# Two homes for turned blocks, rounding steps in rows with gaps, and small operations taken tile by tile

## The chip, the cores and the metric

The kernel runs on one core of a Trainium2 chip. Five engines work side by side, each through its own list of instructions: TensorE (PE; its weight loads are listed as PEld), VectorE (DVE), ScalarE (ACT), GpSimd (POOL) and SyncE (SP), which here issues the DMAs. They wait for one another through semaphores. The metric is the device time of one execution in microseconds; lower is better.

## The reference

Four batches of 256 tokens with 256 features go through four residual stages. In plain form:

```
x = x + xattn0(layernorm(x), ctx, Wq, bq, Wk, bk)      # softmax over ctx, one head
x = x + ternary_ffn(layernorm(x), w_norm, w_gv, w_out)
x = x + xattn1(layernorm(x), ctx, mask, Wq, Wk, Wv, Wo) # 16 heads of 128, 256 keys
x = x + fp8_ffn(layernorm(x), gate, up, down, scales)   # weights rounded to float8_e4m3

# ternary_ffn: weights to {-1, 0, 1} by their mean, activations to 8 bits by their row maximum
scale = 127 / max(max(abs(x)), EPS);  q = clip(round(x * scale), -128, 127) / scale
# fp8_ffn: silu(x @ r(gate) * gs) * (x @ r(up) * us) @ r(down) * ds,  r(w) = w.astype(float8_e4m3fn)
```

## The kernel before, in words

The tokens lie in 8 tiles of 128 rows, two to a batch. Every engine's instructions are issued in an order that is written out by hand as a list of calls; semaphores set what waits for what, and nothing is scheduled by a program.

**The second attention** goes in 32 passes; a pass is one pair of heads of one batch. Its products are split into a high and a low part in a 32-bit format, so that each takes three matmuls (`product`, which records L2016). In a pass TensorE makes queries (`queries`: products of `xT` and `m`), scores (`ctx` and `q`), the product with values (`contexts`: `pT` or `tp` and `cr`) and the output (`attn_out`: `n` and `oT`). VectorE makes the low parts (`q_lo` L1551, `oT_lo` L1595), masks the scores and finds their minimum (L1564), and turns the probabilities; ScalarE takes exponentials and the high parts; POOL normalises and, for the turned passes, subtracts `tp_lo` (L667).

**Turning the probabilities.** In passes 3 to 29 the probabilities get from rows to columns in two steps. VectorE transposes blocks of 32x32 from `sm` to `blocks` (L1581). SP writes `blocks` to a room in DRAM in four DMAs (`blocks_written`, L442) and reads it back as `tp` in two, one for each half of the keys (`blocks_read`, L455; the same issues appear as L454 where a wait is listed). In SP's queue a pass's write and read stand behind those of the pass before. `turns_before(n)` counts the turned passes ahead of pass n; `block_room` and `tp` have two rooms, `blocks` has one. The other passes use TensorE's transposes.

**Rounding to fp8.** The weights are rounded in 16 pieces of 288 columns, spread over the second attention. VectorE takes the exponent bits (L1601) and makes a step of them (L1604); POOL adds the step, subtracts it, and corrects (L672 to L680).

**Small operations.** For each batch the statistics give a mean and a variance for each of its two tiles: one column each, side by side. `stats` negates the means (L1410), `variances` and `second_stats` add an epsilon (L1413, L1461, L1462), `scaled` works out the 8-bit scales of the ternary layer (L1489 to L1495, five dependent steps) and applies them to `gbuf` (L1498), which the first gate product (L2085) waits for. All of them handle both columns in one instruction.

## Time and profile before

| | |
|---|---|
| Median of 3 runs | 310.96 us (310.67 to 313.23) |
| The profiled execution's own time | 312.58 us |
| Its span, first to last instruction | 310.5 us |
| TensorE busy | 293.6 us (95%) |
| VectorE busy | 260.9 us (84%) |
| ScalarE busy | 253.7 us (82%) |
| POOL busy | 218.5 us (70%) |
| Mean granted TensorE clock | 0.995 of 2.4 GHz |

The span counts from the first to the last instruction of the profiled execution; the rest of its time lies around it. Busy shares are means over stages with different limits, so a stage's own stretch has to be read. "Idle before" is put down to what ended last. Matmul records overlap: their ends are modelled, and the distance between two starts is what a step takes in dense work. A few matmul records can be missing.

### The profile page before, as it was taken

What the parts mean: (1) busy time and instruction counts of PE and PEld (TensorE: products, weight loads), DVE (VectorE), ACT (ScalarE), POOL (GpSimd) and SP (SyncE); (2) the same over time, 40 slices, a digit from 0 to 9 for tenths busy, and PEclk for the clock granted to TensorE, in tenths of its full rate; (3) what the DMA queues carried; (4) which work ended last, traced back from release to release, by engine and by line L of the source; (5) the groups of instructions that cost most, each with busy time, mean ns of one, the idle gap of its engine ahead of it and who ended that gap; (6) DMA issues with size and microseconds to landing.
All of it is one profiled execution on the core that took longest, in us unless ns stands there. A gap on an engine that the chain in (4) does not pass through costs nothing.

```text
span 310.5 us, 6396 instructions
## 1 busy us (share of the span) xinstructions
PE 293.6 (95%) x1980; PEld 259.9 (84%) x1992; DVE 260.9 (84%) x713; ACT 253.7 (82%) x603; POOL 218.5 (70%) x290
## 2 busy tenths in 40 slices
PE   3968999999999999999999999999999999999994
PEld 2755487798989998979889999999988999899884
DVE  3959999999999999889999986997768897675665
ACT  2398995598999998979999899778899999855460
POOL 3558864556998578999879998886678798952001
PEclk9979999999999999999999999999999999999999
DMA  7996032001326548885878756537645647200103
GB/s 223 367 381 199 35 101 70 1 8 30 93 47 189 157 138 251 220 212 139 228 210 226 199 144 174 161 108 219 182 144 148 179 143 211 68 3 0 36 1 101
DMA packets 54609, 44.59 MB, mean 144 GB/s; under 512 B 11696, under 2 KB 45104, under 8 KB 54576
## 3 DMA queue, kind: packets, MB, share of 16 engines
q1 hardware_dynamic: 54016, 43.93, 49.0%
q10 hardware_dynamic: 560, 0.26, 0.3%
q8 instruction: 16, 0.26, 0.3%
q14 instruction: 17, 0.14, 0.2%
HBM read 27.01 MB, written 15.20 MB: 136 GB/s over the span
## 4 chain that ended last, share of the span: by engine, by line
PE 59%; DVE 20%; DMA 8%; issue 5%; SPq 4%; ACT 2%; DVEq 0%
PE pb L2016 41%; DMA block_room<-blocks 5%; PE pb L2279 5%; PE pb L2314 4%; DMA wraw<-in_wgvT 3%; DVE blocks L1581 3%; SPq L442 2%; DVE sm L1564 2%; PE pb L2130 2%; PE pb L2091 2%; PE pb L2076 2%; DVE wraw L1455 2%; DVE step L1601 1%; PE pb L2227 1%; DVE q_lo L1551 1%
## 5 line engine op out<-in xcount | busy, mean ns | idle before, releaser
L667 POOL TENSOR_TENSOR tp_lo<-tp,pT_hi 128x512 fp32r<-128x512 f32 x54 | 70.0, 1311 | 15.1 <-ACT pT_hi L993 14.8
L981 ACT ACTIVATE sm<-sm,smin 128x256 f32<-128x256 f32 x128 | 63.6, 501 | 4.7 <-DVE smin L1564 4.4
L1564 DVE CUSTOM_DVE_ANT_0 sm<-pb,mask_all 128x256 f32<-128x256 f32 x128 | 47.3, 418 | 5.6 <-PE pb L2016 5.5
L1581 DVE STREAM_TRANSPOSE blocks<-sm 128x1024 f32<-128x1024 f32 x27 | 33.5, 1240 | 7.4 <-DMA block_room<-blocks 7.0
L2016 PE MATMUL pb<-ctx_hi,q_hi 128*128 128x256 f32 x128 | 38.1, 298 | 1.1 <-DVE q_lo L1551 0.6
L662 POOL TENSOR_SCALAR sm<-sm,srec 128x256 f32<-128x256 f32 x64 | 30.5, 488 | 10.4 <-DVE srec L1570 10.4
L2016 PE MATMUL pb<-xT_hi,m_hi 128*128 128x256 f32 x128 | 37.3, 292 | 0.3 <-DVE xT_lo L1540 0.3
L2016 PE MATMUL pb<-n_hi,oT_hi 128*128 128x256 f32 x128 | 37.1, 290 | 0.2 <-DVE oT_lo L1595 0.2
L2016 PE MATMUL pb<-xT_hi,m_lo 128*128 128x256 f32 x128 | 36.2, 283 | 0.0
L2016 PE MATMUL pb<-xT_lo,m_hi 128*128 128x256 f32 x128 | 36.2, 283 | 0.0
L2016 PE MATMUL pb<-ctx_lo,q_hi 128*128 128x256 f32 x128 | 36.2, 282 | 0.0
L2016 PE MATMUL pb<-ctx_hi,q_lo 128*128 128x256 f32 x128 | 36.1, 282 | 0.0
L2016 PE MATMUL pb<-n_hi,oT_lo 128*128 128x256 f32 x128 | 36.1, 282 | 0.0
L2016 PE MATMUL pb<-n_lo,oT_hi 128*128 128x256 f32 x128 | 36.1, 282 | 0.0
L993 ACT ACTIVATE pT_hi<-tp 128x512 fp32r<-128x512 f32 x54 | 31.7, 622 | 2.4 <-PE pb L2016 2.3
L999 ACT ACTIVATE sm<-sm,srec 128x256 f32<-128x256 f32 x64 | 29.0, 504 | 3.3 <-DVE srec L1570 3.3
L583 POOL TENSOR_TENSOR rstd<-ve,nhalf 128x2 f32<-128x2 f32 (+1 forms) x16 | 13.2, 826 | 21.6 <-DVE ve L1413 18.3
L2016 PEld LDWEIGHTS pb<-ctx_hi,q_hi 128*128 128x128 f32 x128 | 24.4, 191 | 3.6 <-DVE q_lo L1551 2.1
L2016 PE MATMUL pb<-pT_hi,cr_hi 128*128 128x512 f32 x64 | 26.5, 415 | 0.5 <-DVE pT_lo L1591 0.5
L2016 PEld LDWEIGHTS pb<-n_hi,oT_hi 128*128 128x128 f32 x128 | 24.4, 191 | 1.7 <-DVE oT_lo L1595 0.6
L2016 PEld LDWEIGHTS pb<-xT_hi,m_hi 128*128 128x128 f32 x128 | 24.5, 191 | 1.5 <-DVE xT_lo L1540 0.5
L2016 PE MATMUL pb<-pT_hi,cr_lo 128*128 128x512 f32 x64 | 25.3, 395 | 0.0
(195 smaller groups left out, 943.0 us busy)
## 6 DMA issues: line engine op xcount, KB each, us to landing
block_room<-blocks SPq DMA_DIRECT2D x108, 128.0 KB, 2.8
tp<-block_room SPq DMA_DIRECT2D x54, 256.0 KB, 3.0
w_raw<-in_w SPq DMA_DIRECT2D x4, 576.0 KB, 4.6
wraw<-in_wgvT SPq DMA_DIRECT2D x4, 512.0 KB, 8.4
wraw<-in_woutT SPq DMA_DIRECT2D x2, 512.0 KB, 9.3
out<-xb SPq DMA_DIRECT2D x4, 256.0 KB, 2.2
xa<-in_x SPq DMA_DIRECT2D x3, 256.0 KB, 4.5
xb<-in_ctxT SPq DMA_DIRECT2D x2, 256.0 KB, 5.1
```

The costliest lines, as they stand in the source:

```text
L442: sp.dma_start(rows[:, :, i * P:(i + 1) * P], blocks[32 * i:32 * (i + 1), :, :, :].rearrange("a g k b -> a g (k b)")).then_inc(blocks_out, 16)
L583: g.tensor_tensor(rstd[:, planes, tiles(b)], ve[:, planes, tiles(b)], nhalf[:, planes, tiles(b)], ALU.pow).then_inc(rstd_done, 1)
L662: g.tensor_scalar(sm[:, n % 2, k, :], sm[:, n % 2, k, :], srec[:, n % 2, k:k + 1], 1.0, ALU.mult, ALU.mult).then_inc(norm_done, 1)
L667: g.tensor_tensor(tp_lo[:, z, c, :], tp[:, z, c, :], as_f32(pT_hi[:, c, :]), ALU.subtract).then_inc(pT_lo_pool, 1)
L981: a.activation(sm[:, n % 2, k, :], sm[:, n % 2, k, :], ACT.Exp, bias=smin[:, n % 2, k:k + 1], scale=-1.0, accum_out=ssum[:, n % 2, k:k + 1 ...
L993: a.activation(pT_hi[:, c, :], whole, ACT.Copy).then_inc(pT_hi_done, 1)
L999: a.activation(sm[:, n % 2, k, :], sm[:, n % 2, k, :], ACT.Identity, scale=srec[:, n % 2, k:k + 1]).then_inc(norm_act, 1)
L1564: v.tensor_tensor_reduce(out=sm[:, n % 2, k, :], in0=bank(passing_bank("s", 2 * n + h))[:, (k % 2) * S:(k % 2 + 1) * S], in1=mask_all[:, b ...
L1581: v.transpose(blocks[:].rearrange("p g k b -> p k g b"), sm[:, n % 2, :, :].rearrange("p k (g b) -> p k g b", b=32)).then_inc(blocks_done, 1)
L2016: last = t_.matmul(dst, a_, b_, start=start and k == 0, stop=stop and k == n - 1, skip_group_check=check)
L2279: last = t_.matmul(dst, weight[:, k, i * P:(i + 1) * P], part[:, k, tok], start=n == 0, stop=n == 2 * KD - 1)
L2314: last = t_.matmul(bank(DOWN[h][n])[:, t * D:(t + 1) * D], part[:, i, rows], down8[:, i, :], start=i == 0 and t == 0 and part is f_hi, sto ...
```

## The change

- **Turned blocks.** The transposes alternate between `blocks` (even turns) and another room (odd turns): `gbuf` of the ternary layer for the turns before the 17th, and then `uq`, read as 32-bit words. The semaphore of the writes is split in two, one for each room; a transpose waits for the writes of two turns ago, the first odd one for the last use of `gbuf`, the 17th for the last transposes out of `uq`. The two semaphores of the reads become one: SP issues a turn's two reads after both of the turn before have landed, and ScalarE's copies wait for both halves. The first copy of an fp8 gate also waits for the last write out of `gbuf`.
- **Rounding.** `sum8` becomes three rows of 96 columns with one column of gap behind each. VectorE writes the exponent bits there rather than to `step8`, and makes the step from there; POOL's four operations take the same three rows.
- **Small operations.** Those on two columns become two on one column each, 52 more instructions in all; in `scaled`, two tensor-by-tensor products take the second operand as a pointer to one value a row, and the maximum with EPS moves into the first of them. The reciprocal stays on two columns.

```diff
-        sum8 = tile(ctx, "sum8", [P, PIECE])[:]
+        sum8 = tile(ctx, "sum8", [P, 3, PIECE // 3 + 1])[:, :, 0:PIECE // 3]
...
-        blocks_done, blocks_out = sem("blocks_done"), sem("blocks_out")
-        blocks_in = [sem(f"blocks_in{c}") for c in range(SC)]
+        blocks_done, blocks_in = sem("blocks_done"), sem("blocks_in")
+        blocks_out = [sem(f"blocks_out{z}") for z in range(2)]
...
+        UQ_TURN = 17
...
+        def thirds(piece):
+            return piece.rearrange("p (a n) -> p a n", a=3)
...
+        def turned_blocks(k):
+            if k % 2 == 0:
+                return blocks[:]
+            if k < UQ_TURN:
+                return gbuf[:].rearrange("p z t d -> p (z t d)").rearrange("p (g k b) -> p g k b", k=4, b=32)
+            return as_f32(uq[:].rearrange("p a d -> p (a d)")).rearrange("p (g k b) -> p g k b", k=4, b=32)
...
             def blocks_written(n):
...
                 if k >= 2:
-                    sp.wait_ge(blocks_in[0], 16 * (k - 1))
-                    sp.wait_ge(blocks_in[1], 16 * (k - 1))
+                    sp.wait_ge(blocks_in, 16 * SC * (k - 1))
...
-                    sp.dma_start(rows[:, :, i * P:(i + 1) * P], blocks[32 * i:32 * (i + 1), :, :, :].rearrange("a g k b -> a g (k b)")).then_inc(blocks_out, 16)
+                    sp.dma_start(rows[:, :, i * P:(i + 1) * P], turned_blocks(k)[32 * i:32 * (i + 1), :, :, :].rearrange("a g k b -> a g (k b)")).then_inc(blocks_out[k % 2], 16)
...
             def blocks_read(n):
...
-                sp.wait_ge(blocks_out, 64 * (k + 1))
+                sp.wait_ge(blocks_out[k % 2], 64 * (k // 2 + 1))
+                if k >= 1:
+                    sp.wait_ge(blocks_in, 16 * SC * k)
                 for c in range(SC):
-                    if k >= 1:
-                        sp.wait_ge(blocks_in[c], 16 * k)
-                    sp.dma_start(tp[:, k % 2, c, :], block_room[k % 2 * S + c * P:k % 2 * S + (c + 1) * P, :]).then_inc(blocks_in[c], 16)
+                    sp.dma_start(tp[:, k % 2, c, :], block_room[k % 2 * S + c * P:k % 2 * S + (c + 1) * P, :]).then_inc(blocks_in, 16)
...
-                g.tensor_tensor(sum8, raw, step8, ALU.add).then_inc(sum8_done, 1)
+                g.tensor_tensor(sum8, raw, thirds(step8), ALU.add).then_inc(sum8_done, 1)
...
             def probs(n, c):
                 if by_blocks(n):
-                    act.wait_ge(blocks_in[c], 16 * (turns_before(n) + 1))
+                    act.wait_ge(blocks_in, 16 * SC * (turns_before(n) + 1))
...
-                v.tensor_scalar(nmean[:, sl], mv[:, sl, 0], -1.0, None, ALU.mult)
+                for t in range(sl.start, sl.stop):
+                    v.tensor_scalar(nmean[:, t:t + 1], mv[:, t, 0:1], -1.0, None, ALU.mult)
...
             def variances(sl, done):
-                v.tensor_scalar(ve[:, 0, sl], mv[:, sl, 1], EPS, None, ALU.add).then_inc(done, 1)
+                for t in range(sl.start, sl.stop):
+                    ins = v.tensor_scalar(ve[:, 0, t:t + 1], mv[:, t, 1:2], EPS, None, ALU.add)
+                ins.then_inc(done, 1)
...
             def scaled(b):
...
-                scale_next(v.tensor_tensor(hmax[:, sl], hmax[:, sl], rstd[:, 1, sl], ALU.mult))
-                scale_next(v.tensor_scalar(hstep[:, sl], hmax[:, sl], EPS, 1.0 / 127.0, ALU.max, ALU.mult))
+                each = [slice(t, t + 1) for t in range(sl.start, sl.stop)]
+                for one in each:
+                    scale_part(v.tensor_scalar(hmax[:, one], hmax[:, one], rstd[:, 1, one], EPS, ALU.mult, ALU.max))
+                dve.wait_ge(scale_step, scale_count[0])
+                for one in each:
+                    scale_part(v.tensor_scalar(hstep[:, one], hmax[:, one], 1.0 / 127.0, None, ALU.mult))
+                dve.wait_ge(scale_step, scale_count[0])
                 scale_next(v.reciprocal(hrec[:, sl], hstep[:, sl]))
-                scale_next(v.tensor_tensor(hqs[:, sl], hrec[:, sl], rstd[:, 1, sl], ALU.mult))
+                for one in each:
+                    scale_part(v.tensor_scalar(hqs[:, one], hrec[:, one], rstd[:, 1, one], None, ALU.mult))
+                dve.wait_ge(scale_step, scale_count[0])
...
-                if k >= 1:
-                    dve.wait_ge(blocks_out, 64 * k)
-                elif n >= 1:
+                if k >= 2:
+                    dve.wait_ge(blocks_out[k % 2], 64 * (k // 2))
+                elif k == 1:
+                    dve.wait_ge(hq_done, B - 1)
+                else:
                     dve.wait_ge(oT_ps, n)
-                v.transpose(blocks[:].rearrange("p g k b -> p k g b"), sm[:, n % 2, :, :].rearrange("p k (g b) -> p k g b", b=32)).then_inc(blocks_done, 1)
+                if k == UQ_TURN:
+                    for z in range(2):
+                        dve.wait_ge(uq_turned[z], 16 * (NT // 2 - 1))
+                v.transpose(turned_blocks(k).rearrange("p g k b -> p k g b"), sm[:, n % 2, :, :].rearrange("p k (g b) -> p k g b", b=32)).then_inc(blocks_done, 1)
...
-                v.tensor_scalar(step8.bitcast(I32), w8_raw[:, n * PIECE:(n + 1) * PIECE].bitcast(I32), 0x7F800000, None,
+                v.tensor_scalar(sum8.bitcast(I32), thirds(w8_raw[:, n * PIECE:(n + 1) * PIECE]).bitcast(I32), 0x7F800000, None,
                                 ALU.bitwise_and).then_inc(exp8_done, 1)
                 dve.wait_ge(exp8_done, 2 * n + 1)
-                v.tensor_scalar(step8, step8, FP8_LEAST, FP8_STEP, ALU.max, ALU.mult).then_inc(exp8_done, 1)
+                v.tensor_scalar(thirds(step8), sum8, FP8_LEAST, FP8_STEP, ALU.max, ALU.mult).then_inc(exp8_done, 1)
```

The order of TensorE, ScalarE and POOL is as before. On VectorE, where the scales of the first batch are worked out (`hmax`, `hstep`, `hrec`, `hqs`, `gsc`: one column for each tile), it reads before:

```order
L1489 TENSOR_TENSOR hmax<-hmax,rstd 128x2 [waits rstd2_done,gmax_done]
L1490 TENSOR_SCALAR hstep<-hmax 128x2 [waits scale_step]
L1491 RECIPROCAL hrec<-hstep 128x2 [waits scale_step]
L1492 TENSOR_TENSOR hqs<-hrec,rstd 128x2 [waits scale_step]
L1495 TENSOR_SCALAR gsc<-hstep,wmean 128x2 [waits wmean_done,scale_step]
L1498 TENSOR_SCALAR gbuf<-gbuf,hqs 128x256 x2
```

and now:

```order
L1510 TENSOR_SCALAR hmax<-hmax,rstd 128x1 [waits rstd2_done,gmax_done]
L1510 TENSOR_SCALAR hmax<-hmax,rstd 128x1
L1513 TENSOR_SCALAR hstep<-hmax 128x1 [waits scale_step]
L1513 TENSOR_SCALAR hstep<-hmax 128x1
L1515 RECIPROCAL hrec<-hstep 128x2 [waits scale_step]
L1517 TENSOR_SCALAR hqs<-hrec,rstd 128x1 [waits scale_step]
L1517 TENSOR_SCALAR hqs<-hrec,rstd 128x1
L1522 TENSOR_SCALAR gsc<-hstep,wmean 128x1 [waits wmean_done,scale_step]
L1522 TENSOR_SCALAR gsc<-hstep,wmean 128x1
L1526 TENSOR_SCALAR gbuf<-gbuf,hqs 128x256 x2
```

Four of the five steps are now pairs, and each step still waits for the one before. On VectorE where pass 4 is turned (`step`, `sum`: the rounding; `blocks`: the turned block; `q_lo`: low part of the next queries), before:

```order
L1410 TENSOR_SCALAR nmean<-mv 128x2 [waits mv_done]
L1413 TENSOR_SCALAR ve<-mv 128x2
L1601 TENSOR_SCALAR step<-w_raw 128x288 [waits w8_done,ld_eight0]
L1604 TENSOR_SCALAR step<-step 128x288 [waits exp8_done]
L1581 STREAM_TRANSPOSE blocks<-sm 128x4x8x32 [waits blocks_out,norm_done,norm_act]
L1551 SCALAR_TENSOR_TENSOR q_lo<-pb,q_hi 128x512 [waits q_hi_done]
```

and now:

```order
L1422 TENSOR_SCALAR nmean<-mv 128x1 [waits mv_done]
L1422 TENSOR_SCALAR nmean<-mv 128x1
L1426 TENSOR_SCALAR ve<-mv 128x1 x2
L1634 TENSOR_SCALAR sum<-w_raw 128x3x96 [waits w8_done,ld_eight0]
L1637 TENSOR_SCALAR step<-sum 128x288 [waits exp8_done]
L1614 STREAM_TRANSPOSE gbuf<-sm 128x4x8x32 [waits hq_done,norm_done,norm_act]
L1579 SCALAR_TENSOR_TENSOR q_lo<-pb,q_hi 128x512 [waits q_hi_done]
```

The transpose stands at the same place, writes `gbuf` and waits for the ternary layer's `hq_done` rather than for the block's write; later ones wait for `blocks_out0` and `blocks_out1` in turn. SP's queue around the same pass, write and read, before:

```order
L442 DMA block_room<-blocks 32x8x128 [waits blocks_done]
L442 DMA block_room<-blocks 32x8x128 x3
L455 DMA tp<-block_room 128x512 [waits blocks_out,blocks_in0,hq_turned,base_done]
L455 DMA tp<-block_room 128x512 [waits blocks_in1]
L442 DMA block_room<-blocks 32x8x128 [waits blocks_in1,blocks_in0,blocks_done]
L442 DMA block_room<-blocks 32x8x128 x3
L455 DMA tp<-block_room 128x512 [waits blocks_in0,blocks_out,oT_ps]
```

and now:

```order
L452 DMA block_room<-gbuf 32x8x128 [waits blocks_done]
L452 DMA block_room<-gbuf 32x8x128 x3
L465 DMA tp<-block_room 128x512 [waits blocks_out1,blocks_in,hq_turned,base_done]
L465 DMA tp<-block_room 128x512
L452 DMA block_room<-blocks 32x8x128 [waits blocks_in,blocks_done]
L452 DMA block_room<-blocks 32x8x128 x3
L465 DMA tp<-block_room 128x512 [waits blocks_in,blocks_out0,oT_ps]
```

The DMAs keep their order; both reads are released at once, and the next write still stands behind them.

## Rows read from the trace of the kernel before

**Rows 1.** The page, part 1: busy time, share and instructions of each engine.

```profile
PE 293.6 (95%) x1980; PEld 259.9 (84%) x1992; DVE 260.9 (84%) x713; ACT 253.7 (82%) x603; POOL 218.5 (70%) x290
```

**Rows 2.** The page, part 4: the chain that ended last, by engine.

```profile
PE 59%; DVE 20%; DMA 8%; issue 5%; SPq 4%; ACT 2%; DVEq 0%
```

**Rows 3.** Stretches: start:end, length, busy us (x instructions) by engine, PEclk, DMA share, GB/s.

```profile
20.00:76.00 56.00, 53.70 (x351) 42.25 (x352) 53.54 (x148) 47.75 (x94) 36.55 (x52) 0.99 0.26 82
110.00:206.00 96.00, 94.31 (x672) 85.78 (x677) 86.59 (x251) 86.72 (x227) 85.13 (x108) 1.00 0.71 195
206.00:236.00 30.00, 30.00 (x212) 28.05 (x211) 22.94 (x69) 25.94 (x67) 21.79 (x29) 1.00 0.56 157
236.00:242.00 6.00, 5.67 (x35) 4.86 (x34) 5.35 (x7) 5.97 (x16) 4.95 (x6) 1.00 0.60 187
242.00:300.00 58.00, 58.00 (x381) 52.68 (x381) 41.93 (x97) 42.50 (x95) 32.68 (x40) 1.00 0.27 78
```

**Rows 4.** Timeline of TensorE at 122 us: start us, us, operation [idle before <-releaser].

```profile
121.71 0.28 PE L2016 MATMUL pb<-xT_hi,m_lo 128*128 128x256 f32 x1
122.19 0.39 PE L2016 MATMUL pb<-ctx_hi,q_hi 128*128 128x256 f32 x1 [0.20 <-DVE q_lo L1551]
122.42 0.28 PE L2016 MATMUL pb<-ctx_lo,q_hi 128*128 128x256 f32 x1
```

**Rows 5.** Waits of the weight loads: total us, times, longest.

```profile
PEld pb L2016 <- DVE q_lo L1551: 2.1, 4, 0.9
```

**Rows 6.** Waits of VectorE, the transpose.

```profile
DVE blocks L1581 <- DMA block_room<-blocks: 7.0, 9, 1.9
```

**Rows 7.** Waits of SP's queue, the reads.

```profile
SPq L454 <- DMA block_room<-blocks: 33.7, 17, 3.2
```

**Rows 8.** Timeline of SP's queue, the last turn's two reads.

```profile
264.38 0.81 SPq L455 DMA_DIRECT2D tp<-block_room  x2
```

**Rows 9.** VectorE by line: shapes, count, busy us, mean ns, idle before.

```profile
L1601 DVE TENSOR_SCALAR step<-w_raw 128x288 int32<-128x288 int32 x16 | 11.3, 707 | 0.8 <-POOL w8r L680 0.8
L1604 DVE TENSOR_SCALAR step<-step 128x288 f32<-128x288 f32 x16 | 10.4, 649 | 0.6
L1404 DVE BATCH_NORM_STATS2 bnst<-xa 128x6 f32<-128x256 f32 x16 | 5.9, 412 | 4.1 <-DMA xa<-in_x 4.1
L1595 DVE TENSOR_TENSOR oT_lo<-pb,oT_hi 128x512 fp32r<-128x512 f32 x32 | 21.6, 676 | 3.8 <-ACT oT_hi L1005 3.8
```

**Rows 10.** Timelines of VectorE and POOL around 118 us.

```profile
118.29 1.28 DVE L1604 TENSOR_SCALAR step<-step 128x288 f32<-128x288 f32 x1
...
116.80 2.60 POOL L667 TENSOR_TENSOR tp_lo<-tp,pT_hi 128x512 fp32r<-128x512 f32 x2
```

**Rows 11.** POOL, two lines: ns least/median/most, first and last start, shapes.

```profile
L633 POOL TENSOR_SCALAR xa<-gbuf x3: 617/617/617, 38.1 to 77.9; 128x512 bf16<-128x512 f32 x3
...
L639 POOL CAST n_hi<-n_raw x8: 602/610/616, 39.8 to 90.6; 128x512 fp32r<-128x512 f32 x8
```

**Rows 12.** Timeline of VectorE: small operations that start apart.

```profile
25.07 0.17 DVE L1410 TENSOR_SCALAR nmean<-mv 128x2 f32<-128x2 f32 x1
25.15 0.16 DVE L1461 TENSOR_SCALAR ve<-mv 128x2 f32<-128x2 f32 x1
...
43.17 0.20 DVE L1524 TENSOR_SCALAR osc<-ucl,wmean 128x1 f32<-128x1 f32 x1
43.30 0.20 DVE L1521 TENSOR_SCALAR ucl<-umax,gsc 128x1 f32<-128x1 f32 x1
```

**Rows 13.** VectorE, three small lines: ns least/median/most, starts, shapes.

```profile
L1492 DVE TENSOR_TENSOR hqs<-hrec,rstd x4: 160/180/936, 29.9 to 73.9; 128x2 f32<-128x2 f32 x4
...
L1495 DVE TENSOR_SCALAR gsc<-hstep,wmean x4: 228/228/981, 30.1 to 74.8; 128x2 f32<-128x2 f32 x4
...
L1521 DVE TENSOR_SCALAR ucl<-umax,gsc x8: 196/205/216, 42.6 to 178.3; 128x1 f32<-128x1 f32 x8
```

**Rows 14.** Waits of TensorE, the first gate product.

```profile
PE pb L2085 <- DVE gbuf L1498: 0.4, 1, 0.4
```

More of the change, by code:

```diff
@@ L669, in eighths @@
             def eighths(n):
-                raw = w8_raw[:, n * PIECE:(n + 1) * PIECE]
+                raw = thirds(w8_raw[:, n * PIECE:(n + 1) * PIECE])
                 pool.wait_ge(exp8_done, 2 * n + 2)
-                g.tensor_tensor(sum8, raw, step8, ALU.add).then_inc(sum8_done, 1)
+                g.tensor_tensor(sum8, raw, thirds(step8), ALU.add).then_inc(sum8_done, 1)
             def eighths_out(n):
                 pool.wait_ge(sum8_done, n + 1)
-                g.tensor_tensor(sum8, sum8, step8, ALU.subtract).then_inc(step8_done, 1)
+                g.tensor_tensor(sum8, sum8, thirds(step8), ALU.subtract).then_inc(step8_done, 1)
                 pool.wait_ge(step8_done, 2 * n + 1)
-                g.tensor_scalar(step8, sum8, FP8_OVER, 0.0, ALU.mult, ALU.mult).then_inc(step8_done, 1)
+                g.tensor_scalar(thirds(step8), sum8, FP8_OVER, 0.0, ALU.mult, ALU.mult).then_inc(step8_done, 1)
                 pool.wait_ge(step8_done, 2 * n + 2)
-                g.tensor_tensor(w8r[:, n * PIECE:(n + 1) * PIECE], sum8, step8, ALU.add).then_inc(w8_done, 1)
+                g.tensor_tensor(thirds(w8r[:, n * PIECE:(n + 1) * PIECE]), sum8, thirds(step8), ALU.add).then_inc(w8_done, 1)
             def rows4(b):
@@ L1014, in gate4_copy @@
                     act.wait_ge(ld_scales, 48)
+                    act.wait_ge(blocks_out[1], 64 * (UQ_TURN // 2))
                 act.wait_ge(g4_ps, c + 1)
@@ L1460, in second_stats @@
                 stats(xa, sl)
-                v.tensor_scalar(ve[:, 0, sl], mv[:, sl, 1], EPS, None, ALU.add)
-                v.tensor_scalar(ve[:, 1, sl], mv[:, sl, 1], 1.0 + EPS, EPS * EPS, ALU.mult, ALU.add).then_inc(ve2_done, 1)
+                for t in range(sl.start, sl.stop):
+                    v.tensor_scalar(ve[:, 0, t:t + 1], mv[:, t, 1:2], EPS, None, ALU.add)
+                    ins = v.tensor_scalar(ve[:, 1, t:t + 1], mv[:, t, 1:2], 1.0 + EPS, EPS * EPS, ALU.mult, ALU.add)
+                ins.then_inc(ve2_done, 1)
             def centred(b):
@@ L1478, in _, with scale_part, scale_next @@
             scale_count = [0]
-            def scale_next(ins):
+            def scale_part(ins):
                 scale_count[0] += 1
                 ins.then_inc(scale_step, 1)
+            def scale_next(ins):
+                scale_part(ins)
                 dve.wait_ge(scale_step, scale_count[0])
@@ L1488, in scaled @@
                 dve.wait_ge(rstd2_done, b + 1)
-                scale_next(v.tensor_tensor(hmax[:, sl], hmax[:, sl], rstd[:, 1, sl], ALU.mult))
-                scale_next(v.tensor_scalar(hstep[:, sl], hmax[:, sl], EPS, 1.0 / 127.0, ALU.max, ALU.mult))
+                each = [slice(t, t + 1) for t in range(sl.start, sl.stop)]
[5 more added lines that the diff above has]
+                dve.wait_ge(scale_step, scale_count[0])
                 scale_next(v.reciprocal(hrec[:, sl], hstep[:, sl]))
-                scale_next(v.tensor_tensor(hqs[:, sl], hrec[:, sl], rstd[:, 1, sl], ALU.mult))
+                for one in each:
+                    scale_part(v.tensor_scalar(hqs[:, one], hrec[:, one], rstd[:, 1, one], None, ALU.mult))
+                dve.wait_ge(scale_step, scale_count[0])
                 if b == 0:
                     dve.wait_ge(wmean_done, 1)
-                v.tensor_scalar(gsc[:, sl], hstep[:, sl], wmean[:, 0:1], None, ALU.mult).then_inc(gsc_done, 1)
+                for one in each:
+                    ins = v.tensor_scalar(gsc[:, one], hstep[:, one], wmean[:, 0:1], None, ALU.mult)
+                ins.then_inc(gsc_done, 1)
                 for t in range(TB):
@@ L1589, in probs_low @@
                 if n == LAST_TURNED + 1 and c == 0:
-                    dve.wait_ge(blocks_out, 64 * turns_before(n))
+                    dve.wait_ge(blocks_out[0], 64 * ((turns_before(n) + 1) // 2))
                 v.tensor_tensor(pT_lo[:, c, :], bank(passing_bank("pT", SC * n + c)), as_f32(pT_hi[:, c, :]), ALU.subtract).then_inc(pT_lo_done, 1)
```

## The prediction

> **What bounds the kernel now.** I read the page's first list, then its chain of waits, then the busy time by stretches, then the timeline of TensorE and VectorE inside the stretches that lose time. The first list shows TensorE busy for 95% of the span and VectorE, the next, for 84% [rows 1]. The chain that ended last runs over TensorE for 59% and over VectorE for 20% [rows 2]. So TensorE is the bound, and VectorE is what sometimes holds it up. The stretches say where [rows 3]. From 206 to 236 us TensorE is busy for 30.00 of 30, from 242 to 300 for 58.00 of 58: nothing can be won there by freeing another engine. From 110 to 206 us it idles 96.00 − 94.31 = 1.69 us, from 236 to 242 another 0.33: 2.02 us together. From 20 to 76 us it idles 2.30 us while VectorE is busy for 53.54 of 56: there VectorE is nearly full.
>
> A busy row hides part of a stall, since matmul records overlap. In dense work one 128x256 step starts every 0.12 us. At 121.71 the last dense one starts, the next at 122.19 with 0.20 us shown as idle and VectorE's q_lo as the releaser, and the one behind it at 122.42: 0.71 us for what takes 0.24, so 0.47 is lost where 0.20 is shown [rows 4]. I counted nine such gaps between 110 and 242 us; with 0.2 hidden in each the loss is 2.02 + 9 × 0.2 = 3.8 us. The list of waits names q_lo first for the weight loads of the products, 2.1 us [rows 5]; q_lo stands on VectorE right behind the block transpose and the rounding. **So about 3.8 us is what the change can return after 110 us**, however much time VectorE saves.
>
> **Part 1, alternate buffers.** The 27 transposes wait 7.0 us in nine cases for the DRAM writes to have read the one buffer [rows 6]. With two buffers a transpose waits for the writes of two passes ago, which are a whole pass old; these 7.0 us go from VectorE. TensorE cannot have paid all of it, since its whole loss there is 3.8 us. What is late next is SP. Its read of a turn stands in its queue behind the landing of the same turn's write, where it already spends 33.7 us in 17 waits [rows 7], so the next write can still not be issued before. The loop of SP stays as long as it was; the wait leaves VectorE's queue, where q_lo, oT_lo and the scores stood behind it, and stays in SP's, where only the next transfers stand behind it. The two reads of a turn are now released together and ScalarE waits for both. They are issued 0.4 us apart in one pair of 0.81 us [rows 8]: 0 where ScalarE is later than that anyway, 0.4 us once at worst (the last turn). I take 0.
>
> The rooms reused are dead by then, so the first odd turns and the turn that goes to uq wait for work that ended many passes before. The extra wait of the fp8 gate copy is for a write some passes old. Both 0.
>
> **Part 2, the rounding.** The two VectorE steps of a piece take 11.3 + 10.4 = 21.7 us in 32 instructions, 0.707 and 0.649 us in the mean [rows 9]. Many are stretched: the step at 118.29 lasts 1.28 us and ends with POOL's pair of subtractions that runs from 116.80 to 119.40 [rows 10]. The written or read tile now has three rows of 96 with a gap. Bounds for such a step: below, that nothing changes, 0.68 in the mean; above, that it goes at one element per cycle and is no longer held by POOL. The nearest rows of that kind are the statistics of 256 columns, 0.412 us, and the subtraction of 512, 0.676 [rows 9], which never stretch: 0.412 + 32/256 × 0.264 = 0.445 us for 288. I take this, because these rows are nearest in size and the change alters just the shape of the rows that stretch: 32 × 0.445 = 14.2 us, so **−7.5 us on VectorE**; the other end is 0. POOL's three-row forms cost it nothing: its 128x512 step that reads with gaps takes 617 ns, one without 610 [rows 11].
>
> The Trainium skill says the same of the cause in "SBUF — State Buffer", section "Who interferes with whom": VectorE's two-port modes and GpSimd exclude each other on a shared port. Its "VectorE: DVE Perf Modes", section "What auto-detection actually checks", makes that mode hang on outermost counts that are even or equal; 288 against 3 is neither. The stretched row agrees with the first; no row before shows the second.
>
> **Part 3, small operations by tiles.** 52 operations on two columns become 104 on one, so 52 more. Independent ones start 0.08 us apart (25.07, 25.15), those that take a pointer 0.13 (43.17, 43.30) [rows 12]. 40 are of the first kind, 12 of the second, and eight tensor-tensor ones become pointer ones at 0.05 more: 40 × 0.075 + 12 × 0.13 + 0.4 = **+5.0 us on VectorE**. What is removed is their stretching: from the two rows whose longest is furthest above their median, 0.936 − 0.180 and 0.981 − 0.228 make 1.5 us, while the one-column operation stays between 196 and 216 ns in all eight [rows 13]. Between 20 and 76 us lie, for each of four batches, 0.225 in the statistics and 0.49 in the scales, and 0.15 once: +3.0 us, less the 1.5. That is +1.5 on VectorE where it is nearly full. TensorE's idle time there is shared with ScalarE, so I put **+0.5 us** on the path; the ends are −1.5 (only the stretches counted) and +3.0. In the tail, the last statistics are 0.15 later, behind matmuls without a gap [rows 3]: 0.
>
> A rule speaks against this part. The rows show starts 0.08 apart for operations that last 0.17. The Trainium skill, "VectorE: DVE Perf Modes", section "The DRAIN you can't avoid", has the next operation wait until the pipe is empty; by that the 52 would cost 52 × 0.17 = 8.8 us rather than 5.0, as an estimate.
>
> **The sum.** On VectorE −7.0 − 7.5 + 5.0 and the small stretches: about −11 of 260.9 us. On the path, of the 3.8 us after 110 us I take seven tenths, 2.7, because VectorE also waits for ScalarE (3.8 us before oT_lo alone [rows 9]) and would wait there longer. So −2.7 + 0.5 = **−2.2 us**. The profiled execution took 312.58 us for a span of 310.5, the median of the three runs is 310.96; I take the 2.2 from the median: **308.8 us**, 307.3 to 309.9 if the mechanism holds (all of the 3.8 with 0.2 for the early part, or half of it with 0.8).
>
> **The rivals.**
> - *More returns* (18%): all 3.8 us go, and the freed stretches return some 0.7 in the early stage too, where the scales' chain holds TensorE. 310.96 − 4.5 = 306.5. For it: q_lo heads the list of waits. Against: +1.5 on a full VectorE.
> - *TensorE waits for others* (22%): VectorE is free, but the same gaps are then ended by ScalarE, POOL or SP. Between 236 and 242 ScalarE is busy for 5.97 of 6 [rows 3], and SP's loop is not shortened. 311.0.
> - *The gapped step does not do it* (8%): it runs and stretches as before, and only the second buffer works. The waits that matter to TensorE are a few of the nine, about 1.2 us, less 0.5: 310.3.
> - *Slower* (7%): the early chain. From 20 to 76 us VectorE has 2.46 us to spare; if the two-column operations lie in dependent steps that TensorE waits for, the whole +3.0 is paid there, and the later gain is lost to ScalarE: 313.9. It decides from the point where the scales of a batch are what the ternary matmuls wait for; one such wait, 0.4 us for gbuf, is listed already [rows 14]. Beside this, by the skill's rule on the DRAIN, 30 early operations would cost 30 × 0.17 = 5.1 us and the time would be 316; the rows on starts speak against it, and I give it 1 of these 7.
>
> The remaining 45% is my forecast. 1%, some 3.1 us, is about what a measurement of this kernel can tell from no change; so "faster" is below 307.85 and "slower" above 314.07. Faster: nearly all of the first rival and a fifth of the forecast's range, 0.27. Slower: most of the last, 0.05. The range leaves out the far half of the first rival, the last rival and the edge of the second: 306.2 to 311.8.
>
> **What would show it.** In the changed profile: the two rounding steps near 0.445 us each with no long ones beside POOL's subtractions; no wait of the transpose for the DRAM writes, but SP's unchanged; the one-column operations 0.08 and 0.13 apart, with no stretched one, and the scale chains some 0.49 us longer; TensorE's idle between 110 and 206 us below 1 us; POOL's rounding steps still 0.80. If the rounding steps keep means near 0.68, part 2 has failed; if VectorE's waits go and TensorE's idle stays, the second rival holds; if TensorE's idle from 20 to 76 us grows by 2 us or more, the fourth.

## The result, and the profile after

The changed kernel takes 309.41 us in the median (307.88 to 311.58), the kernel before on the same chips 312.25 (310.65 to 313.79), 20 runs each. The ratio is 0.9906, with a 95% interval of 0.9886 to 0.9926: 2.9 us less, where 2.2 were forecast. The profiled execution's span is 307.5 us.

The page of the changed kernel, parts 1 and 4; they answer to [rows 1] and [rows 2]:

```profile
PE 291.3 (95%) x1980; PEld 258.8 (84%) x1992; DVE 254.9 (83%) x765; ACT 253.1 (82%) x603; POOL 215.7 (70%) x290
...
PE 73%; DVE 8%; DMA 6%; issue 4%; SPq 4%; ACT 3%; POOL 2%; DVEq 0%; POOLq 0%
```

VectorE's share of the chain falls from 20% to 8%, TensorE's rises from 59% to 73%. The stretches, columns as in [rows 3]:

```profile
20.00:76.00 56.00, 53.35 (x348) 41.77 (x350) 53.97 (x179) 47.12 (x93) 35.89 (x51) 0.99 0.26 80
110.00:206.00 96.00, 95.57 (x701) 88.80 (x706) 86.07 (x269) 87.47 (x229) 87.44 (x113) 1.00 0.75 196
206.00:236.00 30.00, 30.00 (x199) 27.32 (x198) 22.06 (x61) 28.02 (x72) 21.32 (x28) 1.00 0.63 174
236.00:242.00 6.00, 6.00 (x47) 5.72 (x47) 4.97 (x15) 6.00 (x20) 4.54 (x6) 1.00 0.62 175
242.00:270.00 28.00, 26.79 (x182) 24.38 (x181) 18.31 (x56) 25.47 (x60) 24.01 (x29) 1.00 0.48 133
```

From 110 to 206 us TensorE now idles 0.43 us instead of 1.69, and from 236 to 242 not at all. From 242 to 270, where it had not idled, it idles 1.21. VectorE's lines (shapes, count, busy us, mean ns, idle before) for the two rounding steps, and VectorE's longest entry in the list of waits for a transpose:

```profile
L1637 DVE TENSOR_SCALAR step<-sum 128x288 f32<-128x288 f32 x16 | 7.3, 453 | 0.6
L1634 DVE TENSOR_SCALAR sum<-w_raw 128x288 int32<-128x288 int32 x16 | 7.1, 441 | 1.3 <-POOL w8r L690 1.3
...
DVE blocks L1614 <- issue: 0.8, 2, 0.6
```

The steps cost 14.4 us, against 21.7 in [rows 9] and 14.2 forecast. The 7.0 us of waits for the DRAM writes in [rows 6] are gone. SP still waits for them, as its queue's waits show (us in total, times, longest):

```profile
SPq L463 <- DMA block_room<-blocks: 16.6, 9, 2.8
SPq L463 <- DMA block_room<-gbuf: 14.8, 6, 3.2
SPq L463 <- DMA block_room<-uq: 9.0, 3, 3.6
```

That is 40.4 us for the reads behind the writes, against 33.7 in [rows 7]. In the kernels below that have two rooms it is 34.0 to 40.5 us: SP's loop is no shorter in any of them, as forecast. That the 7.0 us moved there is not shown: e9_best, with 34.0, has no such wait of VectorE either.

**Where the time went, by stages.** ScalarE issues the same 591 operations in the same order in all these kernels. So I compare the starts of five of them, and the span, with the kernel before: the first `cr_hi` (26.61 us before, 25.77 after), the seventh `m_hi` (74.93, 74.83), an exponential (109.91, 109.62), a copy of a gate (260.11, 255.47) and a late `pT_hi` (276.21, 272.88). The differences of those differences are what a stage gains (minus) or loses, in us of one execution:

| kernel | to 27 | 27 to 75 | 75 to 110 | 110 to 260 | 260 to 276 | to the end |
|---|---|---|---|---|---|---|
| changed kernel | −0.85 | +0.74 | −0.18 | −4.35 | +1.32 | +0.31 |
| e1_buffers | −0.43 | 0.00 | 0.00 | −1.98 | −0.01 | −0.02 |
| e2_rounding | −1.29 | +0.89 | +0.03 | +0.33 | −0.18 | +0.25 |
| e3_small | −0.07 | +0.74 | −0.19 | −1.22 | −0.13 | +0.10 |
| e4_halves | −1.79 | +1.06 | −0.19 | −4.58 | −0.14 | +0.33 |
| e5_no_small | +0.04 | −0.04 | +0.03 | −4.24 | +0.04 | +0.21 |
| e6_no_gap | −0.45 | −0.04 | −0.01 | −1.99 | −0.02 | −0.02 |
| e7_short_scales | −1.63 | +0.75 | −0.02 | −4.43 | −0.15 | +0.38 |
| e8_rooms_halves | −1.88 | +0.38 | 0.00 | −1.98 | −0.04 | −0.01 |
| e9_best | −0.13 | +0.32 | +0.03 | −4.34 | −0.16 | +0.22 |
| e10_stats_split | +0.22 | +0.38 | +0.16 | −4.16 | −0.14 | +0.36 |
| e11_merged | −1.46 | +0.48 | +0.02 | −3.47 | +0.66 | +0.25 |
| e12_halves_again | −1.42 | +1.20 | −0.19 | −1.91 | +0.17 | +0.32 |

The first column goes by no part of the change (e5_no_small +0.04, e4_halves −1.79). A few tenths of it are the arrival of the first loads. The larger part goes with VectorE's second operation on the ternary weights (`wraw`), which lasts about 0.7 us in the six kernels that lead by 1.3 us and more, and 1.1 us or more, beside POOL's work on the same tile, in all others; there ScalarE's next `wgv` waits for it. First e6_no_gap:

```profile
22.42 1.23 DVE L1468 TENSOR_SCALAR wraw<-wraw 128x1024 f32<-128x1024 f32 x1
...
23.68 1.15 ACT L945 ACTIVATE wgv<-wraw,minus_round 128x1024 bf16<-128x1024 f32 x1 [1.26 <-DVE wraw L1468]
```

and then e8_rooms_halves:

```profile
20.93 0.69 DVE L1465 TENSOR_SCALAR wraw<-wraw 128x1024 f32<-128x1024 f32 x1
...
21.22 2.22 ACT L942 ACTIVATE wgv<-wraw,minus_round 128x1024 bf16<-128x1024 f32 x2
```

Part of a lead there is lost again in the second column (e2_rounding, e8_rooms_halves, e11_merged, which keep the small operations as they were). The column from 110 to 260 us is where the parts tell, though it too is one execution's: e4_halves and e12_halves_again are the same kernel and lie 2.67 us apart in it.

### The profile page after: what moved, and what is told of

It reads as the page before. It is cut to its first block, busy times and chain, and to the rows that moved or that the text cites. A ratio compares the mean times of both kernels' runs of the same rounds, so it can differ in the third digit from the quotient of the medians.

```text
span 307.5 us, 6450 instructions
## 1 busy us (share of the span) xinstructions
PE 291.3 (95%) x1980; PEld 258.8 (84%) x1992; DVE 254.9 (83%) x765; ACT 253.1 (82%) x603; POOL 215.7 (70%) x290
## 4 chain that ended last, share of the span: by engine, by line
PE 73%; DVE 8%; DMA 6%; issue 4%; SPq 4%; ACT 3%; POOL 2%; DVEq 0%; POOLq 0%
PE pb L2049 52%; PE pb L2312 6%; PE pb L2347 4%; PE pb L2124 3%; DMA wraw<-in_wgvT 3%; PE pb L2163 2%; DMA tp<-block_room 1%; PE pb L2109 1%; DMA block_room<-uq 1%; DMA block_room<-blocks 1%; SPq L465 1%; DVE wraw L1469 1%; SPq L452 1%; PE pb L2260 1%; PE pb L2225 1%
## 5 line engine op out<-in xcount | busy, mean ns | idle before, releaser
L1628 DVE TENSOR_TENSOR oT_lo<-pb,oT_hi 128x512 fp32r<-128x512 f32 x32 | 21.7, 682 | 8.1 <-ACT oT_hi L1015 7.9
```

Source lines behind the costliest of these rows:

```text
L1628: v.tensor_tensor(oT_lo[:, n % 2, :], bank(passing_bank("ctx", n)), as_f32(oT_hi[:, n % 2, :]), ALU.subtract).then_inc(oT_lo_done, 1)
```

## The experiments

All were timed in five rounds; the ratios are to the kernel before on the same chip, with their 95% intervals.

**e1_buffers.** The rooms and their semaphores alone, in the kernel before:

```diff
-                     dve.wait_ge(blocks_out, 64 * k)
+                     dve.wait_ge(blocks_out[k % 2], 64 * (k // 2))
...
+                v.transpose(turned_blocks(k).rearrange("p g k b -> p k g b"), ...
```

> The two rooms alone: the rounding keeps its plain rows and the small operations keep two columns. My theory: the 7.0 us that the transposes wait for the DRAM writes go, the rounding steps still stretch (means near 0.70 and 0.65 us), TensorE loses about 1 to 2 of the 3.8 us after 110 us less, so the ratio to the kernel before is 0.994 to 0.997. Rival, the wait was no one's loss and the rounding alone made the gain: ratio 0.999 to 1.001. Rival, the rooms alone made nearly all of it: 0.986 to 0.991.

0.9916 (0.9884 to 0.9947). The rooms alone return 1.98 us between 110 and 260 us, the upper end of my 1 to 2. The ratio came out below the range that I gave; its interval reaches into it, and holds the changed kernel's 0.9906 too. The one semaphore for both halves of a read costs nothing here: −0.01 us from 260 to 276 us.

**e2_rounding.** The rounding alone, with one room:

```diff
+        sum8 = tile(ctx, "sum8", [P, 3, PIECE // 3 + 1])[:, :, 0:PIECE // 3]
...
-                v.tensor_scalar(step8, step8, FP8_LEAST, FP8_STEP, ALU.max, ALU.mult).then_inc(exp8_done, 1)
+                v.tensor_scalar(thirds(step8), sum8, FP8_LEAST, FP8_STEP, ALU.max, ALU.mult).then_inc(exp8_done, 1)
```

> The rounding in rows with gaps alone: one room for the blocks, small operations on two columns. My theory: both VectorE steps last 0.44 to 0.45 us, none longer; the transposes still wait for the DRAM writes, for more than 7.0 us in total because VectorE arrives earlier; TensorE gets back 1.5 to 2.5 us, ratio 0.992 to 0.995. Rival, the rooms made the gain and VectorE only waits longer here: ratio 0.998 to 1.001 with the transposes' wait at 11 us or more.

1.0028 (0.9997 to 1.0059). My theory falls here: no gain, and between 110 and 260 us a loss of 0.33. The steps did become short (ns least, median, most), and the list of waits tells where that time is:

```profile
L1607 DVE TENSOR_SCALAR step<-sum x16: 452/453/456, 86.3 to 263.9; 128x288 f32<-128x288 f32 x16
...
DVE blocks L1584 <- DMA block_room<-blocks: 20.6, 19, 2.3
```

VectorE reaches its transposes earlier and waits there 20.6 us for the DRAM writes instead of 7.0, as the rival said (11 us or more): the 7.4 us that the rounding saved are in the additional 13.6. With one room, SP's loop of write and read sets when a transpose may run, and `oT_lo` stands behind the transpose. TensorE waits for it 1.6 us, where it waited 0.2 before:

```profile
PE pb L2019 <- DVE oT_lo L1598: 1.6, 2, 1.0
```

**e3_small.** The small operations alone, on one column each:

```diff
-                v.tensor_scalar(nmean[:, sl], mv[:, sl, 0], -1.0, None, ALU.mult)
+                for t in range(sl.start, sl.stop):
+                    v.tensor_scalar(nmean[:, t:t + 1], mv[:, t, 0:1], -1.0, None, ALU.mult)
```

> The small operations by tiles alone. My theory: it costs, +0.3 to +1.0 us, ratio 1.001 to 1.003, all of it between 20 and 76 us, where the first gate product waits 0.9 us for gbuf instead of 0.4. Rival, the stretches that it removes pay for it: ratio 0.997 to 1.000. By the rule that a following operation waits until the pipe is empty it would be 3 us or more: ratio 1.010.

1.0014 (0.9984 to 1.0044), no difference that can be told. In the stages +0.74 us between 27 and 75 us, as expected, and −1.22 later, which I had not expected and which is one execution's. The first gate product waits 0.9 us for `gbuf`, as forecast; that wait alone does not tell the split, since e2_rounding, without it, waits 1.3.

Of the 1.22 us, 0.97 falls between 131 and 137 us, where e1_buffers gains 0.97 of its 1.98. At 130 us a rounding step was held up in the kernel before and not in e3_small, where TensorE also came there 0.5 us later, so that VectorE was in time:

```profile
130.11 1.12 DVE L1601 TENSOR_SCALAR step<-w_raw 128x288 int32<-128x288 int32 x1
...
130.07 0.40 DVE L1618 TENSOR_SCALAR step<-w_raw 128x288 int32<-128x288 int32 x1
```

So part of what the rooms return in these profiles can also come from how the engines fall beside one another in an execution. That the rooms gain on the whole rests on the ratios, 0.9916 against 1.0014 with intervals apart.

**e4_halves.** The changed kernel with a semaphore for each half of a read:

```diff
-        blocks_done, blocks_in = sem("blocks_done"), sem("blocks_in")
+        blocks_done = sem("blocks_done")
+        blocks_in = [sem("blocks_in0"), ld_x[2]]
...
-                    act.wait_ge(blocks_in, 16 * SC * (turns_before(n) + 1))
+                    act.wait_ge(blocks_in[c], 16 * (turns_before(n) + 1 + c))
```

> The changed kernel with one semaphore for each half of a read again (the second half counts on from a semaphore of an early load). My theory: at the last turn ScalarE starts its first copy when the first half has landed, so the 1.4 us that TensorE lost there at 265 us shrink to below 0.9 us and the rest is as in the changed kernel: ratio 0.987 to 0.990. Rival, the queue's loop of write and read is what is late, not the merging: the loss stays within 0.2 us of 1.4 and the ratio is that of the changed kernel, 0.9906.

0.9881 (0.9849 to 0.9913). First the changed kernel at the last turn: SP's reads, ScalarE's copy of what they bring, TensorE's product of it:

```profile
259.75 0.82 SPq L465 DMA_DIRECT2D tp<-block_room  x2
...
264.24 0.63 ACT L1003 ACTIVATE pT_hi<-tp 128x512 fp32r<-128x512 f32 x1 [1.62 <-DMA tp<-block_room]
...
266.27 0.50 PE L2049 MATMUL pb<-pT_hi,cr_hi 128*128 128x512 f32 x1 [1.21 <-POOL tp_lo L677]
```

The copy starts 4.49 us after the reads were issued and the product waits 1.21 us. The two reads were issued 0.38 us apart but landed 1.5 us apart, 3.0 and 4.1 us after their issues:

```profile
L465 SPq DMA_DIRECT2D tp<-block_room x1: 338/338/338, 259.7 to 259.7; - x1
...
DMA to landing us min/median/max: 3.0/3.0/3.0
...
L465 SPq DMA_DIRECT2D tp<-block_room x1: 443/443/443, 260.1 to 260.1; - x1
...
DMA to landing us min/median/max: 4.1/4.1/4.1
```

The same turn in e4_halves:

```profile
258.51 0.81 SPq L467 DMA_DIRECT2D tp<-block_room  x2
...
261.67 0.62 ACT L1005 ACTIVATE pT_hi<-tp 128x512 fp32r<-128x512 f32 x1
...
263.97 0.48 PE L2051 MATMUL pb<-pT_hi,cr_hi 128*128 128x512 f32 x1
```

3.16 us after the issue, and neither of them waits. The loss is gone altogether, where I expected it to shrink below 0.9: in the trace the theory holds and the rival falls. The ratio's interval holds the changed kernel's 0.9906 as well.

**e5_no_small.** Rooms, halves and rounding; the small operations as before:

```diff
                 sl = tiles(b)
-                for one in each:
-                    scale_part(v.tensor_scalar(hmax[:, one], hmax[:, one], rstd[:, 1, one], EPS, ALU.mult, ALU.max))
...
+                scale_next(v.tensor_tensor(hmax[:, sl], hmax[:, sl], rstd[:, 1, sl], ALU.mult))
```

> Two rooms, a semaphore for each half of a read, rounding in rows with gaps; the small operations on two columns as before. My theory now: the rooms release VectorE, and the rounding pays only where the rooms are; splitting the small operations costs up to 0.7 us between 20 and 76 us. So this is as fast as with the split, or up to 0.7 us faster than the run e4_halves: ratio 0.985 to 0.989. Rival, the split pays because two-column operations stretch: ratio 0.990 to 0.993, with scale steps of 0.5 us and more in the trace.

0.9843 (0.9811 to 0.9876), just below the range that I gave and below e4_halves, which was not timed beside it. The scale steps do stretch, as the rival said (ns least, median, most), and yet it is not slower:

```profile
L1505 DVE TENSOR_TENSOR hqs<-hrec,rstd x4: 160/206/945, 29.9 to 73.9; 128x2 f32<-128x2 f32 x4
L1508 DVE TENSOR_SCALAR gsc<-hstep,wmean x4: 228/228/916, 30.1 to 74.8; 128x2 f32<-128x2 f32 x4
```

**e6_no_gap.** The same with rows that touch:

```diff
-        sum8 = tile(ctx, "sum8", [P, 3, PIECE // 3 + 1])[:, :, 0:PIECE // 3]
+        sum8 = tile(ctx, "sum8", [P, 3, PIECE // 3])[:, :, 0:PIECE // 3]
```

> As e5_no_small, but the three rows of 96 lie one behind another without the gap; only the tile's row length differs (96 for 97). My theory: it is the gap that changes the two steps, so they stretch again: means 0.55 to 0.72 us, the longest over 1 us, and the ratio is that of the rooms alone, 0.990 to 0.993. Rival, writing to the other tile is what helped: steps at 0.44 to 0.45 us and the ratio of e5_no_small.

0.9914 (0.9883 to 0.9945). One column of gap decides. Without it the two steps in e6_no_gap:

```profile
L1619 DVE TENSOR_SCALAR sum<-w_raw x16: 260/382/1323, 85.7 to 261.0; 128x288 int32<-128x288 int32 x16
L1622 DVE TENSOR_SCALAR step<-sum x16: 309/474/1432, 86.1 to 262.4; 128x288 f32<-128x288 f32 x16
```

and with it in e5_no_small:

```profile
L1619 DVE TENSOR_SCALAR sum<-w_raw x16: 410/444/454, 86.2 to 259.2; 128x288 int32<-128x288 int32 x16
L1622 DVE TENSOR_SCALAR step<-sum x16: 452/453/455, 86.7 to 259.7; 128x288 f32<-128x288 f32 x16
```

The step with the gap is slower at its best (410 ns against 260) and never slow; without the gap the late stage gains 1.99 us, as with the rooms alone, and with it 4.24. The ratios on the same chip, 0.9914 and 0.9843, have intervals that do not meet: of all runs this one shows most clearly what the rounding is worth beside the rooms.

**e7_short_scales.** e4_halves with one step fewer in the scales and `gsc` behind `gbuf`:

```diff
-                for one in each:
-                    scale_part(v.tensor_scalar(hstep[:, one], hmax[:, one], 1.0 / 127.0, None, ALU.mult))
...
-                scale_next(v.reciprocal(hrec[:, sl], hstep[:, sl]))
+                scale_next(v.reciprocal(hrec[:, sl], hmax[:, sl]))
```

> The run e4_halves with a shorter chain of scales: the step hstep is gone (the factors 127 and 1/127 move into the operations behind it) and gsc is worked out behind the two scalings of gbuf. My theory: gbuf is ready 0.4 to 0.5 us earlier for each batch, the first gate product waits about 0.6 us instead of 1.1, and 0.3 to 0.6 us of it reach the end: ratio 0.986 to 0.988. Rival, another chain is as late there: ratio that of e4_halves, 0.988 to 0.990.

0.9841 (0.9809 to 0.9873). The wait for `gbuf` falls from 1.1 to 0.4 us; the stage from 27 to 75 us is 0.31 better than in e4_halves, though both began with much the same lead. The stage agrees with the theory. The ratio is below the range that I gave and was not taken beside e4_halves; the intervals of the two runs overlap.

**e8_rooms_halves.** Rooms and halves alone; the edit against e5_no_small is the rounding's:

```diff
-                v.tensor_scalar(thirds(step8), sum8, FP8_LEAST, FP8_STEP, ALU.max, ALU.mult).then_inc(exp8_done, 1)
+                v.tensor_scalar(step8, step8, FP8_LEAST, FP8_STEP, ALU.max, ALU.mult).then_inc(exp8_done, 1)
```

> Two rooms and a semaphore for each half, the rounding in plain rows and the small operations on two columns. My theory: the rounding adds 1.5 to 2.5 us where the rooms are, so this is slower than e5_no_small by that: ratio 0.991 to 0.994, with stretched rounding steps and TensorE's gaps at 121 and 154 us of the rooms alone. Rival, the rounding adds nothing here either: within 0.5 us of e5_no_small.

0.9895 (0.9862 to 0.9928) against 0.9843 on the same chip: 0.005 or 1.6 us, with intervals that overlap a little; the ratio itself lies just below the range that I gave. In the stages the rounding adds 4.24 − 1.98 = 2.26 us where the rooms are, and nothing where they are not.

**e9_best, e10_stats_split, e11_merged, e12_halves_again** ran on one chip. The first has the scales of e7_short_scales and the statistics as before; the second only the statistics by tiles; the third is e5_no_small with the one semaphore of the changed kernel; the last is e4_halves again.

```diff
# e9_best, against e7_short_scales; e10_stats_split goes the other way against e5_no_small
-                for t in range(sl.start, sl.stop):
-                    v.tensor_scalar(nmean[:, t:t + 1], mv[:, t, 0:1], -1.0, None, ALU.mult)
+                v.tensor_scalar(nmean[:, sl], mv[:, sl, 0], -1.0, None, ALU.mult)
# e11_merged, against e5_no_small
-                    act.wait_ge(blocks_in[c], 16 * (turns_before(n) + 1 + c))
+                    act.wait_ge(blocks_in, 16 * SC * (turns_before(n) + 1))
```

> Two rooms, a semaphore for each half, rounding in rows with gaps, the statistics on two columns, and the short chain of scales by tiles. My theory: the short chain has fewer steps than either and no stretched one, the statistics cost nothing: ratio 0.982 to 0.986, the fastest of all by a little. Rival, the early stage waits for something else anyway: ratio 0.984 to 0.988, as e5_no_small.

0.9861 (0.9813 to 0.9908), the lowest of the four, within the interval of the others, and so not told apart from the rival's range.

> As e5_no_small, with the statistics' operations alone by tiles (the scales stay on two columns). My theory: the part of the split that costs is the chain of scales, 0.49 us a batch; the statistics cost 0.2 us in all: ratio within 0.001 of e5_no_small, 0.984 to 0.986. Rival, each added operation costs alike and the statistics with 36 of the 52 cost the most: ratio 0.987 to 0.989.

0.9872 (0.9831 to 0.9912): the ratio lies in the rival's range, the interval holds the theory's too. Its stages from 27 to 110 us cost 0.55 more than those of e5_no_small, which speaks for the statistics having a price too.

> As e5_no_small, but with the one semaphore for both halves of a read, as in the changed kernel. My theory: TensorE loses 1.0 to 1.4 us again at the last turn, at 265 us, and nothing elsewhere: ratio 0.988 to 0.990. Rival, the loss at the last turn was that one execution's: no gap over 0.5 us there and the ratio of e5_no_small.

0.9880 (0.9840 to 0.9919). The wait at the last turn is back, 0.94 us on ScalarE and 0.5 on TensorE; it loses 0.66 from 260 to 276 us, less than I expected but the only one beside the changed kernel with more than 0.2 there. Its two reads landed 0.7 us apart (2.7 and 3.0 us after their issues), the changed kernel's 1.5, which is why its loss is the smaller:

```profile
263.77 0.63 ACT L1003 ACTIVATE pT_hi<-tp 128x512 fp32r<-128x512 f32 x1 [0.94 <-DMA tp<-block_room]
```

> The run e4_halves once more, on the chip of the three others: rooms, halves, rounding and all small operations by tiles. My theory: slower than e10_stats_split by 0.4 to 0.9 us, the price of the long chain of scales by tiles, ratio 0.986 to 0.988. Rival, the split costs nothing and the difference to e5_no_small was the chip's: ratio 0.984 to 0.985.

0.9892 (0.9846 to 0.9937), slower than the theory's range. Its profile shows why it is no clean measure of the small operations: the late stage gains only 1.91 us, because TensorE waited for what stands in SP's queue, once for an `oT_lo` whose ScalarE operation stood behind a late read of `tp`, and once for SP's turn of the hidden layer,

```profile
129.65 0.38 PE L2051 MATMUL pb<-n_hi,oT_hi 128*128 128x256 f32 x1 [0.62 <-DVE oT_lo L1630]
...
138.49 1.05 PE L2165 MATMUL pb<-wout,uqT 128*128 128x256 bf16 x8 [1.57 <-DMA uqT<-uq]
```

e11_merged shows the second wait with 0.9 us, e5_no_small and e10_stats_split with 0.2, and e4_halves, the same kernel as this one, neither. With VectorE out of the way, SP's queue is next, in some executions.

## Why the prediction was right, and where its terms were off

**What bounds: right. The cap: too low.** TensorE's gaps between 110 and 242 us behind VectorE were what could be returned. I put the loss at 3.8 us and took seven tenths, 2.7. It was more: 4.35 in the changed kernel, 4.16 to 4.58 in the five others with rooms and rounding and at most 0.2 us of wait for the hidden layer's turn (e4_halves, e5_no_small, e7_short_scales, e9_best, e10_stats_split). So nine gaps with 0.2 hidden in each counted too little, and the reason for the deduction, that VectorE would run into ScalarE's waits, was wrong in its consequence: those waits grew (7.9 us before `oT_lo`, against 3.8 in [rows 9]), but no product of the changed kernel waited for `oT_lo`. In e12_halves_again one did, 0.62 us.

**Part 1: right, and more than its share.** I did not divide the gain between the parts. The rival that only the second buffer works was put at 1.2 us; the rooms without the gapped rounding gave 1.98 or 1.99 in three kernels (e1_buffers, e6_no_gap, e8_rooms_halves). The term that failed is the read's merging. I bounded it by 0.4 us, the distance of the two issues, and took 0. What counts is the distance of the two landings, because the first copy has to wait until the second read has landed as well. It was 0.6 us at the last turn of the kernel before already (2.7 and 2.9 us after the issues), and 1.5 in the changed kernel, where the stage lost 1.32; in e11_merged it was 0.7 and the stage lost 0.66. Nor was there much slack to begin with. In the kernel before, ScalarE reached that copy just as the second read landed, at 267.7 us:

```profile
267.74 0.61 ACT L993 ACTIVATE pT_hi<-tp 128x512 fp32r<-128x512 f32 x1
```

In the changed kernel ScalarE was ready for it at 262.62 us, 5.1 us earlier, while the reads were issued only 4.6 us earlier than in [rows 8]. In e1_buffers the copy did not wait, and nothing was lost. e4_halves shows the cause; how large the loss is differs from one execution to the next.

**Part 2: right in size, and only half the mechanism.** 14.4 us against 14.2 forecast, no stretched step, POOL's wait for the step down from 2.5 us to 0.2. But I summed −7.0 and −7.5 us as if each stood alone. e2_rounding shows that the second is worth nothing without the first, since it turns into the wait that the first removes. The two-port rule of the Trainium skill, "VectorE: DVE Perf Modes", section "What auto-detection actually checks", which I could not show before, agrees with e6_no_gap and e5_no_small: 260 ns at the least where 288 stands against 288, 410 where 288 stands against three rows. The rule on the shared port in the Trainium skill, "SBUF — State Buffer", section "Who interferes with whom", agrees with the longest, 1323 ns against 454. All twelve steps of the kernel before that last over 0.9 us end 0.16 or 0.17 us after an operation of POOL that ran beside them, as the one in [rows 10] does.

**Part 3: right in size.** One chain of scales takes 1.43 us (28.59 to 30.02) instead of 0.96, so +0.47 against 0.49 forecast. The 0.49 came near by luck: it is three pairs of pointer operations and two changes of kind (3 × 0.13 + 2 × 0.05) and leaves out the pair of `hstep`, with which the rows make 0.57. The chain's first and last operation in the kernel before:

```profile
29.29 0.15 DVE L1489 TENSOR_TENSOR hmax<-hmax,rstd 128x2 f32<-128x2 f32 x1
...
30.25 0.76 DVE L1498 TENSOR_SCALAR gbuf<-gbuf,hqs 128x256 f32<-128x256 f32 x2
```

and the timeline of it in the changed kernel:

```profile
28.59 0.32 DVE L1510 TENSOR_SCALAR hmax<-hmax,rstd 128x1 f32<-128x1 f32 x2
28.95 0.22 DVE L1513 TENSOR_SCALAR hstep<-hmax 128x1 f32<-128x1 f32 x2
29.20 0.17 DVE L1515 RECIPROCAL hrec<-hstep 128x2 f32<-128x2 f32 x1
29.40 0.34 DVE L1517 TENSOR_SCALAR hqs<-hrec,rstd 128x1 f32<-128x1 f32 x2
29.77 0.34 DVE L1522 TENSOR_SCALAR gsc<-hstep,wmean 128x1 f32<-128x1 f32 x2
30.02 0.61 DVE L1526 TENSOR_SCALAR gbuf<-gbuf,hqs 128x256 f32<-128x256 f32 x2
```

Two `hstep` take 0.22 us where one takes 0.15: the second starts 0.07 behind the first, as [rows 12] said. The Trainium skill, "VectorE: DVE Perf Modes", section "The DRAIN you can't avoid", says at its head that the next operation does not start until the pipe is empty; this trace does not agree, since by that two of 0.15 would take 0.30. The same section adds that a next operation that is not held starts earlier, which the prediction left out. On the path I put +0.5; the stage from 27 to 75 us lost 0.74 in the changed kernel and in e3_small, of which 0.18 or 0.19 came back by 110 us. How much of the changed kernel's 0.74 is the split and how much a lead lost is open; e3_small began with no lead. No run shows that the stretches which the split removes were worth anything: e5_no_small keeps them and is the faster by ratio, 0.9843 against 0.9881 and 0.9892 of the two runs with the split, though they were not timed side by side and the intervals overlap. e7_short_scales, timed beside it, has the split with a shorter chain and comes to the same, 0.9841.

**The sum.** −2.7 + 0.5 was forecast. The stages give −4.35 + 0.74 − 0.18 + 1.32 + 0.31 = −2.16, and with the 0.85 of the start −3.01: the sum came out by two errors that cancel, a gain put too low by 1.65 and a wait put at 0 that cost 1.32. The +0.31 of the tail I had not foreseen. That the time itself, 309.41, lies so near the 308.8 owes something to a low start as well: I counted from 310.96, the median of three executions, and the twenty put the kernel before at 312.25. As a change the range was −3.7 to −1.1, and the −2.84 between the medians lies in it. Of the rivals, "more returns" had the late stage right and nothing else; "TensorE waits for others" came true at the last turn, and in e12_halves_again behind SP's queue, but the changed kernel's gaps before 242 us closed; "the gapped step does not do it" falls with the 14.4 us; "slower" stood on a price that the rows confirm and that was a quarter as large on the path.

## What to carry to other kernels

A wait that is taken from one engine is worth what the engine's queue behind it is worth, and time saved ahead of a wait goes into the wait: free the buffer first, then shorten the work. Before two signals are merged into one, look at when the two transfers land rather than when they are issued, and at how far their consumer is behind them after the change, not before it. Splitting small operations to keep them from being held up lengthened a chain that others wait for, and no run shows that the holding it removed had cost anything on the path.

## What was not expected of the hardware

A tile with one column of gap went with slower fp8 matmuls: TensorE's 128x512 products of `xT` and `w8r` last 395 or 396 ns in the mean in all nine kernels where `sum8` has rows of 97, and 391 or 392 in the kernel before, e1_buffers, e3_small, e6_no_gap and e8_rooms_halves, where it has not. First the changed kernel (shapes, count, busy us, mean ns, idle before):

```profile
L2312 PE MATMUL pb<-xT_hi,w8r 128*128 128x512 f32 x48 | 19.0, 395 | 0.0
```

and then e6_no_gap:

```profile
L2297 PE MATMUL pb<-xT_lo,w8r 128*128 128x512 f32 x48 | 18.8, 392 | 0.0
```

96 of them at 3 to 4 ns are 0.3 to 0.4 us, the size of the tail's loss of 0.21 to 0.38 in all kernels with the gap, against −0.02 to +0.10 in those without. Whether the tiles placed behind `sum8`, 12 bytes further on, are the cause was not tried.
